# Transposed scores in four PSUM banks in one go, key and value products ahead of them, attends behind the denominators

## The reference, cut to what matters

```python
# for each tile b of 32
y  = clip(modulated_linear(x) + bias, -256, 256)          # 128x128
Q  = (y @ Wq).reshape(128, 4, 4, 64)                      # groups, heads of a group, width
K, V = (y @ Wk).reshape(128, 4, 64), (y @ Wv).reshape(128, 4, 64)
A  = softmax(Q K^T / 8 over the keys) @ V                 # 16 heads
x1 = x + y + A @ Wpost

kx = modulated_linear(x1).reshape(128, 16, 8)             # 16 small heads of width 8
m  = softmax(kx kx^T / sqrt(8), over the 16 heads of the same token) @ kx
t  = modulated_linear(m)

# over all tiles
probs = softmax(t @ gate_w.T)                             # 8 experts, the two best are taken
out   = x1 + sum over experts (gate * (relu(t W1 + b1) W2 + b2))   # full experts are dropped
```

## Time and profile before

| | |
|---|---|
| median of 3 runs | 516.7 us (516.62 to 518.55) |
| profiled execution | 519.01 us, its span 517.0 us |
| PE busy | 499.2 us (97%), 3896 products |
| PE weight loads | 348.6 us (67%) |
| DVE busy | 401.2 us (78%) |
| ACT busy | 371.2 us (72%) |
| POOL busy | 324.0 us (63%) |
| one steady slot | 12.2 us |
| chain that ended last | PE 89%, DVE 5%, ACT 2%, issue 2% |

### The profile page before, as it was taken

How to read it: one execution, slowest core, us unless ns; L and a number is a source line. 1 busy time by engine, 2 the same in 40 slices (tenths; PEclk the granted TensorE clock), 3 DMA queues, 4 the chain that set the end, 5 groups by cost and what they waited for, 6 DMA issues and landing times.

```text
span 517.0 us, 12870 instructions
## 1 busy us (share of the span) xinstructions
PE 499.2 (97%) x3896; PEld 348.6 (67%) x3896; DVE 401.2 (78%) x715; ACT 371.2 (72%) x851; POOL 324.0 (63%) x328
## 2 busy tenths in 40 slices
PE   7899999999999999999999999999999989889997
PEld 6866667666666777766676667666666756666664
DVE  4234788888888888888888888888888797736766
ACT  3467777777777777777777777777777437657873
POOL 1102677777777777777777777777777549004760
PEclk9999999999999999999999999999999989999999
DMA  6500000000000000000000000000000000000004
GB/s 221 155 1 2 2 1 2 1 0 0 0 0 0 0 0 0 0 0 0 0 0 0 0 0 0 0 0 0 0 0 2 1 1 0 2 0 2 0 21 143
DMA packets 9364, 7.19 MB, mean 14 GB/s; under 512 B 1088, under 2 KB 8832, under 8 KB 9216
## 3 DMA queue, kind: packets, MB, share of 16 engines
q1 hardware_dynamic: 9344, 6.94, 4.6%
HBM read 4.84 MB, written 2.10 MB: 13 GB/s over the span
## 4 chain that ended last, share of the span: by engine, by line
PE 89%; DVE 5%; issue 2%; ACT 2%; DMA 1%; SPq 1%; POOL 1%; DVEq 0%; ACTq 0%; POOLq 0%
PE bank_a L704 11%; PE misc L711 11%; PE bank_d L719 11%; PE bank_t L686 11%; PE bank_s L671 7%; PE bank_d L696 6%; PE bank_t L953 4%; PE bank_t L681 4%; PE misc L841 3%; PE misc L843 3%; PE misc L808 2%; PE bank_s L961 2%; PE bank_d L961 2%; PE misc L868 1%; PE bank_a L642 1%
## 5 line engine op out<-in xcount | busy, mean ns | idle before, releaser
L1374 POOL TENSOR_TENSOR pair<-kx 128x1152 f32<-128x1152 f32 x32 | 82.9, 2591 | 96.6 <-DVE shifted L422 77.7
L300 DVE TENSOR_REDUCE row_max<-bank_s 128x4 bf16<-128x512 f32 x128 | 89.4, 699 | 67.7 <-PE bank_s L671 67.7
L1339 POOL TENSOR_TENSOR mix_hi<-mix_hi 128x512 f32<-128x512 f32 (+2 forms) x96 | 79.7, 831 | 3.1
L1007 ACT ACTIVATE qT<-misc 128x512 f32<-128x512 f32 x64 | 39.1, 611 | 53.7 <-PE misc L711 53.6
L1007 ACT ACTIVATE prob<-bank_t 128x512 f32<-128x512 f32 x128 | 69.7, 603 | 4.4 <-PE bank_t L686 2.8
L719 PE MATMUL bank_d<-attT,wpost_sb 128*128 128x128 f32 x512 | 69.2, 278 | 0.2 <-DVE attT L308 0.2
L711 PE MATMUL misc<-yT,wq_sb 128*128 128x128 f32 x512 | 67.7, 275 | 0.0
L704 PE MATMUL bank_a<-prob,v 128*32 128x512 f32 x512 | 67.4, 598 | 0.0
L686 PE MATMUL bank_t<-qT,kT 64*128 64x256 f32 x512 | 65.7, 376 | 0.0
L1345 POOL TENSOR_TENSOR mix_hi<-weight,kx 128x1024 f32<-128x1024 f32 x32 | 63.1, 1973 | 0.3 <-ACT weight L1007 0.3
L711 PEld LDWEIGHTS misc<-yT,wq_sb 128*128 128x128 f32 x512 | 62.2, 192 | 0.8
(11 more groups left out here) (183 smaller groups left out, 934.9 us busy)
## 6 DMA issues: line engine op xcount, KB each, us to landing
out<-acc_all SPq DMA_DIRECT2D x8, 256.0 KB, 2.3
x_all<-in_xT SPq DMA_DIRECT2D x1, 1024.0 KB, 9.7
w_sb<-in_w SPq DMA_DIRECT2D x2, 512.0 KB
x_all<-in_xT SPq DMA_DIRECT2D x1, 768.0 KB, 7.6
wq_sb<-in_wq SPq DMA_DIRECT2D x1, 512.0 KB, 6.2
wpost_sb<-in_wpost SPq DMA_DIRECT2D x1, 512.0 KB, 9.8
x_all<-in_xT SPq DMA_DIRECT2D x1, 256.0 KB, 3.2
b_rows<-in_b SPq DMA_DIRECT2D x16, 4.0 KB
```

Source lines behind the costliest of these rows:

```text
L300: V.tensor_reduce(bass.AP(row_max, first_w * (P + 1) + HPG * p, [[HPG * P, P], [P + 1, 2], [KEY, 2], [1, 1]]), bank_s[:, :, :].rearrange(" ...
L1007: return nc.scalar.activation(out_, in_, func, **kw)
L1339: G.tensor_tensor(mix_hi[:, jd, 0:r, :], mix_hi[:, jd, 0:r, :], mix_hi[:, jd, r:2 * r, :], ALU.add).then_inc(s_hi, 1)
L1374: G.tensor_tensor(pair[:, :, :], bass.AP(kx2, jc * 2 * P, [[4 * P, P], [0, SHIFTS], [1, P]]), bass.AP(kx2, jc * 2 * P, [[4 * P, P], [MD, S ...
```

## The change

- `scores_t` writes p = 0 into the two `bank_t` and p = 1 into the two `bank_a` (`wide_a`). Its waits change accordingly: p = 0 for the exponentials of the tile before and for `kx2` of the tile before, p = 1 for the normalised values of the tile before.
- `keys` and `keys_turned` use `bank_t[0]` and wait for the first exponential (`s_prob`).
- PE's order in a slot: queries 0, first output product, `scores` 3, tokens, second output product, transposed maxima, key and value products, both `scores_t`, `scores` 0, queries 1, `keys`, `scores` 1, the next tile's product, denominators, both attends, `keys_turned`, `scores` 2, `mixing_turned`.
- DVE, ACT and POOL get a new order too. No product, copy or transfer is added or removed; `gate_logits` and `keep_going` move along.

```diff
--- before.py
+++ after.py
@@ -159,12 +159,13 @@
 
         bank_x = [b[:, :].rearrange("p (t f) -> p t f", f=P) for b in bank_a] + [misc[1][:, :, :]]
 
+        wide_a = bank_x[0:2]
         bank_e = [bank_s, bank_d]
         bank_b = bank_x[0:2] + [misc[0][:, :, :], misc[1][:, :, :]]
 
         def key_out(b):
 
-            return misc[1][:, 0:1, :] if s_is(b, BATCH - 1) else bank_x[1][:, 0:1, :]
+            return misc[1][:, 0:1, :] if s_is(b, BATCH - 1) else bank_t[0][:, 0:1, :]
 
         def mix_out(b):
 
@@ -464,29 +465,29 @@
                     V.tensor_tensor(x_all[:, col(c)], bank_d[:, 0, :], x_all[:, col(c)], ALU.add).then_inc(s_x1T, 1)
 
                 def loop_slot():
-                    if B:
-                        heads_max(s, 3)
                     if C:
                         normalise(c, 1)
                     if D:
                         weight_sums()
+                    if B:
+                        heads_max(s, 3)
+                    head_scores()
+                    if C:
+                        attended()
+                    if D:
                         weight_inverses()
                         weighted_rows()
-                    if C:
-                        attended()
-                    head_scores()
+                    if A:
+                        heads_max(a, 0)
                     if D:
                         row_sum()
+                    if D:
+                        rows_joined()
+                    mixed()
                     head_maxima()
                     if A:
-                        heads_max(a, 0)
                         heads_max(a, 1)
-                    if D:
-                        rows_joined()
                     head_shift()
-                    mixed()
-                    if A:
-                        heads_max(a, 2)
                     if has(a + 1):
                         dve.wait_ge(s_y_raw, n(a + 1))
                         need(dve, s_kv_mm, n(a))
@@ -496,6 +497,8 @@
                         count_ahead()
                     if B:
                         normalise(s, 0)
+                    if A:
+                        heads_max(a, 2)
                     if s_is(s, BATCH - 1):
                         normalise(s, 1)
 
@@ -674,16 +677,21 @@
 
             def scores_t(s, j, p):
 
-                need(pe, s_prob, 4 * s + 2 * p)
+                if p == 0:
+                    need(pe, s_prob, 4 * s)
+                    need(pe, s_kx2, s - 1)
+                else:
+                    need(pe, s_attT, 2 * s)
                 pe.wait_ge(s_neg, n(s))
+                bank = (bank_t, wide_a)[p]
                 for half in range(2):
                     rows = slice(KEY * half, KEY * (half + 1))
-                    mm(bank_t[half][:, :, :], g_rows[rows, 2 * p + half, :], neg_diag[rows, j, :, :],
+                    mm(bank[half][:, :, :], g_rows[rows, 2 * p + half, :], neg_diag[rows, j, :, :],
                        start=True, stop=True, skip_group_check=True)
                 for w in range(0, HPG, 2):
                     for half in range(2):
                         rows = slice(KEY * half, KEY * (half + 1))
-                        last = mm(bank_t[half][:, w:w + 2, :], kT[rows, j, p, :], qT[rows, j, p, w:w + 2, :],
+                        last = mm(bank[half][:, w:w + 2, :], kT[rows, j, p, :], qT[rows, j, p, w:w + 2, :],
                                   start=False, stop=True, skip_group_check=True)
                         if w == HPG - 2:
                             last.then_inc(s_t_mm, 1)
@@ -760,6 +768,8 @@
 
                 x, q = unit(u)
                 need(pe, s_ah, u - 1)
+                if u == 0:
+                    pe.wait_ge(s_kx2, BATCH - 1)
                 if q == QUADS - 1:
                     pe.wait_ge(s_tok, BATCH)
                 pe.wait_ge(s_ah_w1, x + 1)
@@ -792,6 +802,8 @@
 
                 def keys(b):
                     pe.wait_ge(s_x1s, n(b))
+                    if has(b + 1):
+                        pe.wait_ge(s_prob, 4 * b + 5)
                     mm(key_out(b)[:, 0, :], modw_sb[:, 1, :], x1s[:, :], start=True, stop=True).then_inc(s_kx_mm, 1)
 
                 def keys_turned(b):
@@ -810,10 +822,6 @@
                 def loop_slot():
                     if s_is(s, -1):
                         keep_going(8)
-                    if final:
-                        gate_logits(parts_early[0])
-                    if B:
-                        scores(s, j, 3)
                     if A:
                         pe.wait_ge(s_yT, n(a))
                         queries(a, 0)
@@ -822,19 +830,17 @@
                             pe.wait_ge(s_ld_post, 32)
                         posts(c, 0)
                     if B:
+                        scores(s, j, 3)
+                    if has(d - 1):
+                        tokens_made(d - 1)
+                    if C:
+                        posts(c, 1)
+                    if B:
                         pe.wait_ge(s_max, 4 * n(s))
                         for w in range(HPG):
                             last = mm(bank_s[:, w, :], row_max[:, w, :], ident16[:, :],
                                       start=(w == 0), stop=True, skip_group_check=True)
                         last.then_inc(s_neg_mm, 1)
-                    if C:
-                        posts(c, 1)
-                    if s_is(s, 0):
-                        keep_going(5)
-                    if B:
-                        scores_t(s, j, 0)
-                    if has(d - 1):
-                        tokens_made(d - 1)
                     if A:
                         pe.wait_ge(s_q, 2 * a + 1)
                         for i in range(2):
@@ -843,10 +849,12 @@
                         mm(misc[0][:, 2:4, :].rearrange("p a f -> p (a f)"), yT[:, :], wv_sb[:, :], start=False,
                            stop=True, skip_group_check=True).then_inc(s_kv_mm, 1)
                     if final:
+                        gate_logits(parts_early[0])
                         gate_logits(parts_early[1])
-                    if C:
-                        keys(c)
+                    if s_is(s, 0):
+                        keep_going(5)
                     if B:
+                        scores_t(s, j, 0)
                         scores_t(s, j, 1)
                     if s_is(s, -1):
                         keep_going(6)
@@ -861,15 +869,15 @@
                     if final:
                         gate_logits(parts_early[2])
                         gate_logits(parts_early[3])
+                    if C:
+                        keys(c)
+                    if A:
+                        scores(a, ja, 1)
                     if has(a + 1):
                         if A:
                             pe.wait_ge(s_v, n(a))
                         pe.wait_ge(s_xs, n(a + 1))
                         mm(misc[0][:, 0, :], modw_sb[:, 0, :], xs[:, j, :], start=True, stop=True).then_inc(s_y_mm, 1)
-                    if C:
-                        keys_turned(c)
-                    if A:
-                        scores(a, ja, 1)
                     if s_is(s, -1):
                         keep_going(6)
                     if B:
@@ -877,16 +885,15 @@
                             pe.wait_ge(s_x1T, n(c))
                         denominators(s)
                         attend(s, j, 0)
+                        attend(s, j, 1)
+                    if C:
+                        keys_turned(c)
                     if A:
                         scores(a, ja, 2)
                     if D:
                         if A:
                             pe.wait_ge(s_q, 2 * n(a))
                         mixing_turned(d)
-                    if B:
-                        if C:
-                            pe.wait_ge(s_kx2, n(c))
-                        attend(s, j, 1)
                     if final:
                         pe.wait_ge(s_neg, BATCH)
                         pe.wait_ge(s_rt, ROUTE_STEPS["count1"])
@@ -1026,7 +1033,7 @@
 
                 act.wait_ge(s_t_mm, 4 * s + g + 1)
                 need(act, s_av_mm, 2 * s)
-                f(prob[:, g, :, :], bank_t[g % 2][:, :, :], ACT.Exp, scale=KEY_SCALE).then_inc(s_prob, 1)
+                f(prob[:, g, :, :], (bank_t + wide_a)[g][:, :, :], ACT.Exp, scale=KEY_SCALE).then_inc(s_prob, 1)
 
             def copy_q(b, j, half):
                 act.wait_ge(s_q_mm, 2 * b + half + 1)
@@ -1178,19 +1185,15 @@
                     return
                 if A:
                     copy_q(a, ja, 0)
+                    narrow_q(a, ja, 0)
                 if B:
                     act.wait_ge(s_neg_mm, n(s))
                     need(act, s_t_mm, 4 * n(s - 2))
                     f(neg_diag[:, j, :, :], bank_s[:, :, :], scale=-1.0).then_inc(s_neg, 1)
-                if A:
-                    narrow_q(a, ja, 0)
+                if has(d - 1):
+                    tokens_out(d - 1)
                 if C:
                     x1_scaled()
```

(36 more changed lines are left out.)

## The result

The changed kernel takes 526.3 us, median of 4 (523.46 to 529.26), against 516.66 for the kernel before beside it (516.52 to 518.55): ratio 1.018, 95% interval 1.010 to 1.026. The same program run again gave 523.86 (523.43 to 526.04), ratio 1.014 (1.009 to 1.018). I had forecast 516.2 with a range up to 520, so the prediction was wrong. The profiled execution of after took 523.48 us around a span of 521.6, which is 4.6 more than the span before.

The account below looks back on a forecast made before the run. PE was taken as the bound before, then a two-slot loop through POOL and VectorE (24.33 us); opening −1.3, steady slots −1.6 and end +2.4 gave −0.5, so 516.7 became 516.2 us, range 510.5 to 520.

Parts of the forecast that it names:

- Strip sets: On PE, two of four strip sets a slot go, saving 0.46 us a slot (bounds 0.20 to 0.60).
- Banks and exponentials: Four exponentials in a row on ScalarE end at 8.4 us, before PE's denominators at 8.57; 0.1 to 0.2 us to spare.
- rival 3: Slower: strip exits or late exponentials hold PE between first query product and keys' transpose; round 24.7, 521.2 us; chance 0.20.
- The loop that closes: Round from PE through keys' transpose, POOL, VectorE and yT to PE: 24.33 us for two slots, 12.17 a slot.
- The opening: Opening slots, before the head mixing exists: 3 × 0.46 saved, less the loop's first closing, about −1.3 us.
- End, the pick: At the loop's end, `pair` and POOL's next product delay VectorE's three expert-picking products: +2.4 us (bounds 0 to +3).
- Rivals 1 and 2: The first: PE stays the bound, slots of 11.77, 505.3 us, chance 0.05. The second: see rival 2.
- rival 2: The shorter loop, POOL and VectorE alone, rules: 11.97 a slot, 509 to 511.5 us; chance 0.22.

Follow-up runs that it names:

- `mixing_behind`: Changed kernel with `rows_joined` and `mixed` behind yT on DVE and PE's `mixing_turned` and `tokens_made` in the next slot; median 512.55 us, ratio 0.989.
- `half_sum`: Changed kernel with DVE's `row_sum` adding 4 of its 8 rows, the other 4 left out of the mixing; median 524.28 us, ratio 1.012.
- `turned_early`: Changed kernel with the keys' transpose between the denominators and the first attend; median 521.8 us, ratio 1.008.
- `both_cut`: Changed kernel with the keys' transpose between denominators and attend and `row_sum` over 4 of 8 rows, together; median 514.42 us, ratio 0.994.
- `end_turned_early`: Changed kernel with the keys' transpose moved between denominators and attend in slot 31 only; median 521.75 us, ratio 1.010.
- `gate_first`: Changed kernel with the gate's first part back at the head of slot 31, in front of the queries; median 522.41 us, ratio 1.011.
- `combined`: Changed kernel with `mixing_behind`, `gate_first` and `end_turned_early` together; median 509.41 us, ratio 0.983.

## Why the prediction was wrong, step by step

**Strip sets: right.** Denominators to attend 0.88, the second lot of transposed scores 209.41 − 208.32 = 1.09 behind the first, as forecast. With both loops out of the way (`mixing_behind`) the whole order gives 0.32 of the 0.46 a slot.

**Banks and exponentials (the place of rival 3): held.** The denominators never wait for `prob` in the steady slots; their start, 212.46, is 8.62 behind the first query product, where I had laid out 8.57.

**The loop that closes: the step that failed.** I closed one loop, over POOL and two slots, and sized it 24.33 (12.17 a slot). The term is mis-sized: it is 24.66 (12.33 a slot), already longer than two slots of the kernel before. Such a loop exists twice, one for each of the two slots of a round, and the two are not alike. The longer one in after: transpose to `pair` 203.95 − 202.99 = 0.96 (forecast 0.85), `pair` to last halving 9.70 (9.59), to DVE 0.10 (0.04), `rows_joined` to `head_shift` 1.72 (1.78), to yT and PE 0.33 + 0.50 (0.71), query product to transpose 11.33 (11.36). Together 24.64, and two slots take 24.66: nothing in it waits for anything else. In the other one the transpose is followed by `pair` after 0.86 and yT by the query product after 0.34, and `rows_joined` comes 0.38 behind the last halving, so it has room. The mean of the two, 24.5, hides the one that binds. In `half_sum`, where DVE's row sum is out of the way, the hops of the longer one are 0.97, 9.71, 0.10, 1.71, 0.33, 0.51 and 11.33, 24.66 again, and the slot is 12.33.

The second fault is a loop that is not in the prediction at all. It closes in one slot between PE and DVE: first query product to the next `scores` 0 on PE, 210.58 − 203.84 = 6.74; to the maxima on DVE 0.43; `heads_max` 0.61; `row_sum` 2.02 to `rows_joined`; 1.71 to `head_shift`; 0.33 to yT; 0.34 and 0.50 in turn, 0.42 in the mean, to the next query product. Sum 12.26, and `turned_early`, where POOL never holds up `rows_joined`, has a slot of 12.27. (In the slot shown `row_sum` to `rows_joined` is 2.13; 0.11 of it is the wait for POOL.) I had seen that yT now stands behind POOL's work, and not that it stands behind `row_sum`, 2 us of DVE's own work that begins only when PE has given the next slot's scores. Before the change `row_sum` had run by then: the head maxima that stood behind it began at 223.87, ahead of the first maxima of the next slot. This loop alone would have cost 0.04 a slot against the kernel before even if the one over POOL had had the forecast length. `half_sum`, `turned_early` and `both_cut` together show both: 12.33 with the loop over POOL alone, 12.27 with the one between PE and DVE alone, 12.03 with neither.

**So the steady slots** cost +2.61 where I had −1.6: 4.2 us, the largest part of the miss. 24.66 lay inside the bounds that I had given the loop (23.94 to 24.8), but my range for the median did not carry them to its upper end.

**The opening** gave 0.79 and not 1.3. No run tells which hop took the rest.

**End, the pick: right.** Its three products in after:

```profile
418.45 1.46 DVE L360 TENSOR_TENSOR t<-key 128x64 f32<-128x64 f32 x1
...
420.20 1.63 DVE L363 TENSOR_TENSOR t<-index,place 128x64 f32<-128x64 f32 x1
421.87 1.30 DVE L365 TENSOR_TENSOR t<-t,index 128x64 f32<-128x64 f32 x1
```

From `h_den` to the third product's end 417.52 to 423.17 = 5.65, against 3.48 before (415.44 to 418.92): +2.2, forecast +2.4, and `end_turned_early` takes 2.1 of it back here (3.57), and 2.4 of the whole end. POOL meanwhile:

```profile
417.26 2.57 POOL L1376 TENSOR_TENSOR pair<-kx 128x1152 f32<-128x1152 f32 x1 [7.48 <-ACT kx L1014]
419.78 1.97 POOL L1354 TENSOR_TENSOR mix_hi<-weight,kx 128x1024 f32<-128x1024 f32 x1
```

The first product of the pick ends at 419.91 and `pair` at 419.83, the second at 421.83 and POOL's product at 421.75: each lasts as long as the POOL instruction beside it. The Trainium skill (SBUF — State Buffer, SBUF: two separate sides) says that a VectorE operation with two SBUF inputs and a GpSimd operation that reads SBUF hold the shared ports exclusively, whoever starts first; these rows agree with it.

**End, the clock: missed.** Another 1.7 us came from the denominators and attends of slot 31 at half the granted clock. I had no term for it; the kernel before has 1.00 in the same stretch.

**The median.** The forecast of −0.5 became +4.6 in the profiled spans: +0.5 opening, +4.2 steady slots, +1.6 end, −1.3 loads. The medians are 9.6 apart because the profiled execution of before was 2.3 above its own median and that of after 2.8 below. The four executions of after were 523.5 and 529.2 us long, two each, with mean granted clocks of 0.993 and 0.980. Before the second set I expected these two lengths again and nothing between; it gave 523.43, 523.71, 524.01 and, at a clock of 0.986, 526.04. So there are not two lengths: the length goes with the clock. That set, 523.86 against 517.41 in 15 executions of before, gives +6.5.

**The rivals.** Rival 3 had the right sign, nearly the right size (521.2) and the right round: it was to decide from 24.46 on, was priced at 24.7, and 24.66 came. But what it gave as the reason, late exponentials and exits from strips between query product and transpose, was not at work: that hop was 11.33, shorter than forecast, and the round grew in the others. It had no term for the clock either, so its nearness to the median is in part luck. Rivals 1 and 2 fell (the terms of rival 2 add up to 511.0 at most, not 511.5), though rival 2's shorter loop, 12.04 when measured, is what comes next once both longer ones are cut. Of the signs I had named, the attends at 0.88, the scores at 1.09, PE's wait in front of the query product, POOL's idle time put down to `kx` and the stretched pick all came. DVE's wait for POOL in front of `mix_sum` is listed in few slots (2.8 us in 6 waits), because `row_sum` ended only 0.04 ahead of the last halving or behind it, and that was the sign of the missed loop.

## What to carry to other kernels

When a step is moved behind others on one engine, list every loop that now passes through the waiting instruction, the short ones in one slot too, and add up each from the other engine's trigger on; the long loop that looks dangerous may have a shorter twin of nearly the same length. A loop that spans several slots exists in as many copies, and hops may differ from slot to slot: add up each copy by its own hops, for the mean hides the one that binds. Cutting one of two nearly tied loops shows little, so before a theory is dropped, cut both at once. What shortens the bounding engine pays only when nothing that it feeds is put in front of its own next start.

## What was not expected of the hardware

- Behind the 22 eight-column products of the gate, the clock granted to PE fell to 0.57 of full over 412 to 416 us in after, so to its level of 1.2 GHz for most of it. It fell ahead of the picked experts' products in the profiles of all kernels here but two, the one before and `gate_first`; in `combined`, which has the gate in the order of `gate_first`, it fell all the same. So the order of the gate's products is not shown to be the cause. What decides is open. In the kernel before it fell only later, to 0.57 over 421 to 425 us, behind PE's wait of 2.53 us.
- Executions of one program differ by the clock: after took 523.4 to 524.0 us at a mean of 0.993, 526.0 at 0.986, 529.1 and 529.3 at 0.980.
- From yT's start to the first query product passed 0.34 us in one slot (203.50 to 203.84) and 0.50 in the next (215.80 to 216.30), where the rolled loop begins a new round. On a loop that binds this counts in full.
- The stall on POOL moved with DVE's weighted rows: `xs` 1.38 before is 0.40 now, and `score` L1366, 0.42 before, is 1.40 beside DVE's `mix_lo` (208.37 for 1.93). From `pair` to the last halving POOL takes nearly as long as before (9.59 and 9.70); the 0.11 more are a third of what the loop grew by over the forecast.
